# Three step groups in place of five, a group's last list ordered by levels, and shared experts placed elsewhere, in a macaron layer on one core

## What is computed

```python
x = x + 0.5 * ffn(layernorm(x))         # layer 0
x = x + attention(layernorm(x))
x = x + 0.5 * ffn(layernorm(x))         # layer 1, same weights

def attention(x):       # 8 x 512 rows of 128, windows of 128 rows
    q, k, v = x @ Wq.T + bq, x @ Wk.T + bk, x @ Wv.T + bv
    scores = q @ k.T / sqrt(128)
    # all but the 32 largest of each row are masked; softmax; @ v
    # leaky relu of it, + x, layer norm with gamma and beta

def ffn(x):             # 4096 rows, layer norm first
    # 8 experts, the two with the largest logits of a row are taken
    # gates: softmax of those two probabilities
    # expert: silu(x @ Wg.T) * (x @ Wu.T) @ Wd.T, 128 -> 384 -> 128
    # one shared expert for all rows, 128 -> 128 -> 128
    return sum(gate * expert(x)) + shared(x)
```

## Time and profile before

| | us |
|---|---|
| median of three runs | 567.1 (565.56 to 568.05) |
| the profiled execution | 561.75 |
| its span, first to last instruction | 559.8 |

### The profile page before, as it was taken

One profiled execution on the slowest core, in us unless ns is written; L12 is line 12 of the kernel. 1 busy time (PEld: TensorE's weight loads), 2 busy tenths in 40 slices (PEclk: granted clock), 3 DMA queues, 4 the chain that ended last, 5 costly groups with the idle time before them and its releaser, 6 DMA issues.

```text
span 559.8 us, 14467 instructions
## 1 busy us (share of the span) xinstructions
PE 494.4 (88%) x3928; PEld 455.7 (81%) x3928; DVE 389.0 (69%) x1704; ACT 329.1 (59%) x792; POOL 291.7 (52%) x328
## 2 busy tenths in 40 slices
PE   2657979998999999999999888699999999999790
PEld 1644979987888999979899686689999999999780
DVE  5354754663357899997989999999987635422674
ACT  3472656643376677866776675586675555754440
POOL 2270477767637543326547325616667763764442
PEclk9987999999999999999999898899999999999996
DMA  6954567687667656558443471245577678786994
GB/s 176 323 132 145 184 191 260 241 253 179 218 229 261 233 189 219 178 173 311 166 153 132 151 241 63 100 172 197 208 224 242 218 248 276 256 286 217 323 303 149
DMA packets 88012, 117.82 MB, mean 210 GB/s; under 512 B 11848, under 2 KB 60880, under 8 KB 87936
## 3 DMA queue, kind: packets, MB, share of 16 engines
q1 hardware_dynamic: 76208, 96.75, 52.2%
q0 software_dynamic: 9312, 19.16, 9.9%
q10 hardware_dynamic: 2416, 0.99, 0.7%
HBM read 26.57 MB, written 26.19 MB: 94 GB/s over the span
## 4 chain that ended last, share of the span: by engine, by line
PE 64%; DVE 12%; DMA 10%; SPq 5%; issue 4%; ACT 3%; POOL 0%; ACTq 0%; DVEq 0%; POOLq 0%
PE ps_g L740 14%; PE ps_y L754 14%; PE ps_u L745 7%; PE ps_h L745 7%; DMA raw_gu<-rows 4%; PE ps_x L735 3%; DMA raw_dn<-in_dnw 3%; PE w L702 2%; PE w L684 2%; PE w L685 2%; PE w L650 2%; PE w L635 1%; SPq L505 1%; PE w L644 1%; SPq L491 1%
## 5 line engine op out<-in xcount | busy, mean ns | idle before, releaser
L1600 POOL DMA_INDIRECT results<-raw_gu x163 | 162.7, 998 | 159.4 <-ACT raw_gu L954 117.4
L1589 POOL DMA_INDIRECT rows<-zz,s_idx x128 | 123.9, 968 | 98.6 <-DVE s_idx L1204 41.0
L754 PE MATMUL ps_y<-dn_t,raw_gu 128*128 x978 | 139.7, 279 | 4.5 <-ACT raw_gu L954 3.3
L740 PE MATMUL ps_g<-x_t,raw_dn 128*128 128x128 f32 x978 | 138.5, 279 | 0.0
L754 PEld LDWEIGHTS ps_y<-dn_t,raw_gu 128*128 128x128 f32 x978 | 123.5, 193 | 12.4 <-issue 11.7
L740 PEld LDWEIGHTS ps_g<-x_t,raw_dn 128*128 128x128 f32 x978 | 124.4, 194 | 4.2 <-issue 4.0
L954 ACT COPY raw_gu<-ps_y 128x128 f32<-128x128 f32 x163 | 43.0, 264 | 92.1 <-PE ps_y L754 89.4
L948 ACT ACTIVATE sil<-ps_g 128x384 f32<-128x384 f32 x163 | 79.9, 490 | 22.5 <-PE ps_g L740 21.6
L945 ACT ACTIVATE x_t<-ps_x,bf_c,gf_c 128x128 f32<-128x128 f32 x163 | 75.4, 463 | 16.8 <-PE ps_x L735 16.5
L745 PE MATMUL ps_u<-x_t,raw_dn 128*128 128x128 f32 x492 | 69.6, 278 | 1.7 <-DVE raw_gu L1413 1.7
L1413 DVE TENSOR_TENSOR raw_gu<-sil,ps_u 128x384 f32<-128x384 f32 x82 | 45.1, 549 | 37.1 <-PE ps_u L745 24.8
(11 more groups left out here) (215 smaller groups left out, 692.6 us busy)
## 6 DMA issues: line engine op xcount, KB each, us to landing
raw_dn<-gu_t SPq DMA_DIRECT2D x163, 384.0 KB
raw_gu<-rows SPq DMA_DIRECT2D x163, 64.5 KB
yg<-results SPq DMA_DIRECT2D x15, 512.0 KB, 4.6
results<-raw_gu POOLq DMA_INDIRECT x163
rows<-pads SPq DMA_DIRECT2D x40, 64.5 KB
rows<-pads SPq DMA_DIRECT2D x5, 451.5 KB
rows<-zz,s_idx POOLq DMA_INDIRECT x128
out<-xres SPq DMA_DIRECT2D x7, 256.0 KB, 3.2
```

The source lines that it names most:

```text
L740: t = pe.matmul(ps_g[k][:, c, :], ws[:, k4, c * P:(c + 1) * P], x_t[:, k, :], start=True, stop=True)
L754: t = pe.matmul(ps_y[:, 0, :], h_t[:, k4, c * P:(c + 1) * P], dn[:, bass.ds(off + c * D, D)], start=(c == 0), stop=(c == FC - 1))
L1589: pool.indirect_dma_start(xs, bass.IndirectOffsetOnAxis(s_idx[n][:, c, k:k + 1], 0), zz[n][:, k, c, :], None).then_inc(scat[n], 16)
L1600: pool.indirect_dma_start(yt, bass.IndirectOffsetOnAxis(xin[:, ky, D:D + 1].bitcast(I32), 0), yb[:, ky, :], None).then_inc(yst[ky], 16)
```

## The change

Three groups in place of five: steps 0 and 1 of layer 0, steps 2 to 7 of layer 0, and all of layer 1, so 149 blocks. The lists have 23 and 55 blocks in layer 0, and 9, 8, 8, 8, 8, 8 and 22 in layer 1. A last list is now ordered by levels: blocks that hold only rows of steps below 3 first, then below 4, 6 and 8 (layer 1: below 7, then 8). Results of a level's steps are loaded when its blocks are stored (`complete`), and the list has 8 times as many bins as there are levels. Layer 1 ends with one step behind level 7. No step is prepared alone. Shared experts 0 to 3 stand ahead of the blocks, in banks that the blocks use later; 4 and 5 at the head of the turn that prepares step 4, 6 and 7 at the head of the turn that prepares step 6. There are four result buffers in layer 1 in place of two, the new ones in the tiles of scores and keys. The weave is another one.

```diff
-GROUPS = ((3, 3, 2), (7, 1))
-LISTS = ((2, 3, 6, 8), (2, 4, 5, 6, 7, 8))
+GROUPS = ((2, 6), (8,))
+LISTS = ((2, 8), (2, 3, 4, 5, 6, 7, 8))
+LEVELS = (2,), (3, 4, 6, 8), (7, 8)
-LATE = (3,)
+LATE = ()
-AHEAD = 2
+EARLY = 4
+def complete(ph, to):
+    first = next(f for f, p in zip(FIRST, PHASE) if p.group == PHASE[ph].group)
+    return first + 2 * TB * (to - PHASE[ph].lo) + SPARE
+READY_AT = tuple(to for levels in LEVELS[:len(GROUPS[0])] for to in levels)
+READY_OF = tuple(sum(to <= J for to in READY_AT) for J in range(STEPS))
+def shared_turns():
+    for f in TURNS:
+        first = f.a if f.a in LATE else f.p
+        starts = first and READY_OF[first] != READY_OF[first - 1]
+        yield tuple(R for R in range(EARLY, STEPS) if starts and READY_OF[R] == READY_OF[first])
...
+        banks_early = (ps_g[0], ps_u, ps_h), (ps_g[1], ps_x, ps_y), (ps_g[0], ps_u, ps_h), (ps_g[1], ps_y, ps_h)
...
             def results(C, n, tile):
-                sp.wait_ge(cb, C * N_CB + N_CB)
+                if C < STEPS + 2:
+                    sp.wait_ge(cb, C * N_CB + N_CB)
+                elif C < STEPS + 4:
+                    sp.wait_ge(sc_sb, STEPS)
+                    apart(sp)
+                    sp.wait_ge(pr_done, (STEPS + 1) * TB)
+                else:
+                    sp.wait_ge(cb, (C - 1) * N_CB)
...
-                    stored(ph)
-                    for J in range(PHASE[ph].lo, PHASE[ph].hi):
-                        results(layer * STEPS + J, J % 2, J * TB)
-                        if layer and J:
-                            output(STEPS + J - 1, J * TB - TB)
+                    for lo, to in itertools.pairwise((PHASE[ph].lo,) + LEVELS[PHASE[ph].group]):
+                        if layer and lo == LAST_LO:
+                            break
+                        stored(complete(ph, to))
+                        for J in range(lo, to):
+                            results(layer * STEPS + J, yg_of(layer * STEPS + J), J * TB)
+                            if layer and J >= 3:
+                                output(STEPS + J - 3, (J - 3) * TB)
...
+            def shared_between(R, begun, mixed, done):
+                pe.wait_ge(sc_sb, begun)
+                pe.wait_ge(q_sb, begun)
+                pe.wait_ge(k_sb, begun)
+                pe.wait_ge(v_sb, begun + 1)
+                pe.wait_ge(o_sb, mixed + 1)
+                pe.wait_ge(xr_done, SHARED_NO[R] + 1)
+                pe.wait_ge(shh, SHARED_NO[R] + 1)
+                prefixes_read(done)
+                shared_both(R, nz_first[R])
...
+            first_turn(0)
+            first_logits(0)
+            first_turn(1)
+            first_prefixes(0)
+            first_logits(1)
+            first_turn(2)
+            first_logits(2)
+            first_prefixes(1)
+            first_prefixes(2)
+            first_up(0)
+            first_up(1)
+            first_down(0)
+            first_up(2)
+            first_turn(3)
+            first_logits(3)
+            first_down(1)
+            first_up(3)
+            first_prefixes(3)
+            first_down(2)
+            first_down(3)
+            for R in range(4, STEPS):
+                first_turn(R)
                 first_logits(R)
+                first_prefixes(R)
...
+                for n in SHARED_AT[s]:
+                    shared_between(n, a, turned - (A is not None), done)
+                    turn()
+                    shared_down(n)
+                    turn()
...
+                if f.last:
+                    if f.first:
+                        link(dve.tensor_copy(edge[:, 0:NE], region(g)))
+                    else:
+                        link(dve.scalar_tensor_tensor(edge[:, 0:NE], listed[:, 0:NE], float(P), region(g), ALU.mult, ALU.add))
+                    rows_upto(run[:], bins // NE, link)
+                    link(dve.tensor_tensor(nbk[:, 0:bins], edge[:, NE:bins + NE], edge[:, 0:bins], ALU.subtract))
...
+                link(dve.tensor_tensor_scan(bend[:, 0:bins], one_f[:, 0:bins], nbk[:, 0:bins], 0.0, ALU.mult, ALU.add))
+                link(dve.tensor_tensor(cell, starts, every(bend[:, 0:bins]), ALU.is_ge))
+                link(dve.tensor_reduce(be[:, 0:nb], cell, AX_X, ALU.add))
+                if f.last:
+                    link(dve.tensor_scalar(be[:, 0:nb], be[:, 0:nb], NE - 1, None, ALU.bitwise_and))
+                link(dve.tensor_tensor(cell, cell, every(skip[:, 0:bins]), ALU.mult))
+                link(dve.tensor_reduce(bs[:, 0:nb], cell, AX_X, ALU.add))
```

More of the change, by code:

```diff
@@ L815, in _ @@
                 if p is not None:
[L816 removed]
+                    turn_x(p % XRING, p, joined)
                     turn()
@@ L1293, in after_step @@
             def after_step(layer, J):
+                for ph in range(PHASES):
+                    f = PHASE[ph]
+                    if f.layer == layer and f.last and J + 1 in LEVELS[f.group][:-1]:
+                        level(1 + LEVELS[f.group].index(J + 1))
                 for ph in range(PHASES):
```

306 lines of the change are left out of this document (173 added, 133 removed).

## The result

| | before | after |
|---|---|---|
| median of the runs | 566.16 us (5 runs, 564.84 to 568.05) | 556.82 us (5 runs, 555.04 to 560.08) |
| ratio, 95% interval | | 0.9854, 0.9813 to 0.9896 |
| the profiled execution, its span | 561.75, 559.8 us | 560.08, 558.3 us |

The change makes the kernel 1.5% faster, where the forecast was 4.1%. The profiled execution is the slowest of its five runs, and that of before is faster than all five of the table, so the two spans show 1.5 us where the medians show 9.3; the stages are compared here, the medians give the size.

A forecast was written before the change was run, and what follows sets the result against it. GpSimd's indirect DMAs were taken to bound the start, VectorE the middle, then TensorE, DMA and VectorE the tail. Block 141 stored at 502 plus a tail of 35 made a span of 537 us, and 7.3 more 544; range 526 to 559.

The forecast's parts named there:

- the start: Up to score copy 0: combine 0 at about 142, 25 us earlier, and score copy 0 at 157 us.
- Start, GpSimd before: Kernel before, up to combine 0: 95 indirect DMAs at 1.26 us plus 19.0 idle from 23.25, giving 162.0 us.
- Start, GpSimd after: Changed kernel, up to combine 0: 87 DMAs, 109.6 us, done at 132.9, plus 3 for waits and 5 for landing and load.
- Start, TensorE: TensorE's early blocks: through block 22 at about 118 us, then idle 6 us until block 23 at about 124.
- Blocks: Whole kernel: 149 blocks instead of 163, so 14 x 2.12 = 29.7 us of TensorE work go.
- The wide list at nothing: VectorE's 32-bin list in layer 0: about 8 us, hidden under step 7's scatter, taken as nothing; bounds nothing and 8 us.
- Turns: Between the layers: score copy 3 at about 250, score copy 7 about 375, last routing about 446; experts add 6 and 8 us.
- End and tail: After the last routing: last 22 blocks from 466 to 512, block 141 stored about 502, tail 35 us, span 537.
- Signs named ahead: Trace marks: right if combine 0 at 138 to 147, last routing 438 to 452; wrong if block 23 after 135.
- 2 (the early start carries through, 531): From the start to the last routing: level 6 is no gate, last routing about 438, time 531; chance 0.20.
- 5 (block 23 waits): Step 7's scatter in layer 0 ends late, block 23 waits to 147 or later, kernel slower, 573 at 153; chance 0.04.
- The Trainium skill: Two page rules, left out: half clock after new waits, sum some 5 us longer; VectorE holding GpSimd up by 4 us.

The follow-up runs named there:

- e1: The changed kernel with ten chained memsets on GpSimd ahead of step 7's scatters: 562.25 us, 0.9925 of the kernel before.
- e8: The changed kernel with the 1760-cell comparison of the 55-block list made three times instead of once: 559.44 us, 0.9894 of the kernel before.
- e3: The changed kernel without the shared experts of steps 4 to 7 of layer 0, their places in the turns kept: 552.3 us, 0.9763 of the kernel before.
- e7: The changed kernel with two result buffers in layer 1 in place of four: 561.9 us, 0.9945 of the kernel before.

## Why the prediction was right and wrong

It had the sign, and the measured 556.8 lies in its range (526 to 559) around 544. But of the 23 us of gain that it forecast 9.3 came, and the stretches show that most of the rest is missing in the start. The sum of the profiled execution can be laid beside it:

| stretch | forecast | after | difference |
|---|---|---|---|
| to score copy 0 | 157 | 174.1 | +17.1 |
| to score copy 3 | 93 | 91.7 | -1.3 |
| to score copy 7 | 125 | 128.7 | +3.7 |
| to the last routing | 71 | 69.0 | -2.0 |
| to the end | 91 | 94.8 | +3.8 |
| span | 537 | 558.3 | +21.3 |

From the span to the median 7.3 us were added; here the profiled execution is 3.3 us above its median, so that of the 21.3 us 12.8 remain in the medians.

**The step that failed is the start**, in its two halves: "combine 0 at about 142, 25 us earlier", which came at 156.9, 10 us earlier; and "PE is through block 22 at about 57 + 23 x 2.2 + 10 = 118, so it idles 6 us", where TensorE reaches block 23 at 136.2 and does not wait for it at all.

- **Start, GpSimd before**: the premise that GpSimd's queue set combine 0 was wrong. By the trace 84 DMAs and not 95 end with the last result needed, at 152.5 and not 162.0, and combine 0 did not wait for its load. That the sum met a row at 162.31 was luck, and bad luck, since it seemed to confirm the count. Some 10 of the 25 us were never there to be gained.
- **Start, GpSimd after**: the 87th DMA ended at 142.4 for 132.9 + 3. New waits were 10.2 us for 3, as steps 1 and 3 are routed too late for it; the two long scatters add 2.4; the first scatter came 2.8 sooner. "Landing and load take 5 us as before" was 14.5 us to combine 0, as before 14.3: SyncE issues the load only at 152.0, behind weights and rows of blocks. "Landing and reading" of block 23, put at 3 us, is 5.4 (e1).
- **Start, TensorE**: costed up to block 22, with 60.6 us from block 0 on and not one wait. It took 83.2, from 53.0: 68.4 of work and 14.8 of waits, for VectorE behind the list, for ScalarE, for an early expert. From block 23 to score copy 0 there were 33 us in the forecast (124 to 157) and 37.9 in the trace, of which 34.0 are work. Score copy 0 itself was never costed by TensorE's count, only by adding 15 us to a time of GpSimd's. With rows at 133.5 the same 37.9 us give 171, an estimate: GpSimd's chain alone would have cost 14 of the 17 us, and TensorE's, which came 3 us later, all of them.
- **Blocks**: 149, and 266 matmuls fewer, which is 14 x 19. TensorE's busy time fell by 21.7 us and not by 29.7; a matmul's record is 129 ns long on average for 126. Why stays open.
- **The wide list at nothing**: wrong. Each operation took 1.99 us as forecast, but the product behind two of them held TensorE up by 3.15 us, and e8 prices 4 us more of list at about 2 us of the whole, near the limit of what a measurement tells. That it would be "under step 7's scatter" was true of GpSimd and not of TensorE.
- **Turns**: as forecast in their lengths, partly by luck. Experts 4 and 5 cost 5 to 6 us, as forecast (6). Experts 6 and 7 cost 3 us or less by e3, where 8 were taken, and VectorE's pace there is 125.8 us without them, where 118 were taken: two errors that cancel.
- **End and tail**: the forecast 35 us from the first load to the end are 32.2 (526.1 to 558.3), and e7 shows 5 us for the four buffers. The load itself comes 62.7 us after the last routing, where 56 were forecast.
- **Signs named ahead**: of the right ones only the 149 blocks, the missing 19 us gap and the spacing of the seven combines came. Combine 0, score copy 3, the last routing and layer 1's first combine (530.7) all missed their windows, and two of the wrong ones came true: block 23 after 135 and the last routing near 465.
- **Rivals**: 2 (the early start carries through, 531) has its mechanism shown and its premise not: starts do carry through, but it wasn't early. 5 (block 23 waits) is the direction in which it went; block 23 came at 136 of the 147 needed to lose all, but by TensorE's and GpSimd's chains together.
- **The Trainium skill**: both of its pages bear on what happened, and both had been left out of the sum. The page "TensorE: Matmul & The Clock Gate", section "What's actually happening": after the wait of 3.15 us six matmuls take 1.65 and 1.49 us in place of 0.83, at a granted clock of 0.83 over 100 to 120, some 3 us lost. The trace agrees with the rule but not with the 5 us or the places drawn from it: before block 23 there is no wait, from 266 to 395 the clock is 0.97 as it was before (0.96), and over the whole span it is 0.969 for 0.970. The page "SBUF — State Buffer", section "Who interferes with whom": the two scatters under two-input operations lose 0.95 and 1.40 us, and those under e8's added comparisons as well, while one under a reduction of the same length loses nothing. The 2.4 us are in GpSimd's sum above.

What it would take to gain more was tried in part: none of the orders tried beats the changed kernel by more than a measurement can tell. By the tie above that would need both chains of the start shortened at once, which no run did.

## What to carry to other kernels

A sum that meets a row of the trace to 0.3 us is no proof: count the instructions up to that row, and look whether the one that it is to explain waited at all. Here 11 scatters were counted too many, and combine 0 had no wait. When a stall of one engine goes, add up what every other engine has to do up to the same mark, with its waits, before taking the gain: TensorE reached block 23 at 136 where its bare work had been put at 118. A wide operation on an in-order engine is paid by whoever waits for the short one queued behind it, however well it is hidden under a third engine. And a wait of the busiest engine can make the work behind it slower as well: here six matmuls took 1.65 us in place of 0.83.

## What was not expected of the hardware

An indirect DMA with a median of 0.96 us took 1.72 to 2.64 us when it started under a VectorE operation of 2 us with two tile inputs, in every profile of the changed kernels; a reduction of 1760 cells left it at 0.96. From the end of the last scatter on GpSimd to the issue of the load that depends on it took 3.4 us (e1), and the rows came 2.1 us after that.
